# Attention with the fourth step added by a transfer from five probability buffers, and SP's reciprocal work split in two

## The reference

```python
h = _sln(hidden, w, ln_g, ln_b, Wg, bg, Wb, bb)
qkv = (h @ Wqkv.T + bqkv).reshape(B, N, num_heads, hd, 3)      # B 4, N 1024, 16 heads of 32
energy = jnp.einsum('bhqd,bhkd->bhqk', q, k)
att = jax.nn.softmax(energy, axis=-1) / D ** 0.5               # D 512
out = jnp.einsum('bhqk,bhkd->bhqd', att, v)
out = out @ Wp.T + bp
h1 = out + hidden
return _sln(h1, ...) + h1
```

## Time and profile before

| | us |
|---|---|
| median of 3 runs | 1867.25 |
| lowest, highest | 1859.41, 1867.28 |
| profiled execution | 1867.83 |
| its span, first to last instruction | 1865.7 |
| TensorE matmuls busy in the span | 1815.0 |
| VectorE, GpSimd busy | 1252.1, 1217.5 |

### The profile page before, as it was taken

One profiled execution on the slowest core, in us unless ns is written; L12 is line 12 of the kernel. 1 busy time (PEld: TensorE's weight loads), 2 busy tenths in 40 slices (PEclk: granted clock), 3 DMA queues, 4 the chain that ended last, 5 costly groups with the idle time before them and its releaser, 6 DMA issues. The chain is left out here.

```text
span 1865.7 us, 27084 instructions
## 1 busy us (share of the span) xinstructions
PE 1815.0 (97%) x9510; PEld 1214.0 (65%) x9510; DVE 1252.1 (67%) x1986; ACT 836.4 (45%) x1547; POOL 1217.5 (65%) x681
## 2 busy tenths in 40 slices
PE   8999999999999999999999999999999999999897
PEld 4678888888888788888555545554555555454376
DVE  4655655655655565556887777777777777777387
ACT  3223123122223122221476666666666666666465
POOL 2665465465464243332588888888988888898565
PEclk9999999999999999999999999999999999999999
DMA  7410110210103657595877778777878787865796
GB/s 271 118 35 23 57 34 22 56 34 22 56 1 118 209 206 244 180 292 181 199 164 175 184 167 184 175 181 177 182 179 185 172 182 170 185 153 133 232 383 235
DMA packets 135373, 287.10 MB, mean 154 GB/s; under 512 B 23984, under 2 KB 41520, under 8 KB 127200
## 3 DMA queue, kind: packets, MB, share of 16 engines
q1 hardware_dynamic: 102996, 200.10, 35.8%
q0 software_dynamic: 9264, 66.11, 17.4%
q10 hardware_dynamic: 23008, 19.54, 3.3%
HBM read 134.68 MB, written 84.19 MB: 117 GB/s over the span
## 5 line engine op out<-in xcount | busy, mean ns | idle before, releaser
L1619 DVE TENSOR_REDUCE at_mrow<-banks 128x1 f32<-128x512 f32 x976 | 594.1, 681 | 163.7 <-PE banks L1465 163.6
L1715 POOL TENSOR_TENSOR at_sums<-at_probs 128x2048 f32<-128x2048 f32 x127 | 596.6, 4698 | 91.5 <-DMA at_sums<-at_sums 80.2
L1599 ACT ACTIVATE at_probs<-banks 128x512 f32<-128x512 f32 x1024 | 519.7, 621 | 182.7 <-PE banks L1483 177.4
L1465 PE MATMUL banks<-early_ks,early_qs 96*128 96x512 f32 x976 | 407.9, 418 | 11.0 <-DVE at_mrow L1619 7.1
L1483 PE MATMUL banks<-early_qs,early_ks 98*128 98x512 f32 x1024 | 408.0, 417 | 1.8 <-ACT at_probs L1599 1.8
L1465 PEld LDWEIGHTS banks<-early_ks,early_qs 96*128 96x128 f32 x976 | 184.8, 189 | 145.1 <-DVE at_mrow L1619 91.6
L1483 PEld LDWEIGHTS banks<-early_qs,early_ks 98*128 98x128 f32 x1024 | 193.7, 190 | 105.6 <-ACT at_probs L1599 81.5
L1495 PE MATMUL banks<-at_probs,at_v 128*32 128x512 f32 x2048 | 249.1, 603 | 0.7 <-DMA at_v<-v_scratch 0.7
L66 PE MATMUL banks<-l_nt,l_weights 128*128 128x512 f32 x768 | 179.4, 394 | 5.4 <-DVEq L1193 4.3
L66 PE MATMUL banks<-l_ht,l_weights 128*128 128x512 f32 x768 | 178.9, 393 | 1.9 <-issue 1.9
L657 ACT ACTIVATE l_gt<-banks,mod 128x512 f32<-128x512 f32 x60 | 45.1, 778 | 299.3 <-PE banks L526 263.5
(11 more groups left out here) (147 smaller groups left out, 2155.3 us busy)
## 6 DMA issues: line engine op xcount, KB each, us to landing
at_sums<-at_sums POOLq DMA_DIRECT2D x63, 1024.0 KB, 8.3
qk_scratch<-qk_out SPq DMA_DIRECT2D x64, 512.0 KB, 6.1
early_ks<-qk_scratch SPq DMA_DIRECT2D x48, 512.0 KB, 5.2
early_qs<-qk_scratch SPq DMA_DIRECT2D x96, 256.0 KB, 5.7
attn_scratch<-at_out SPq DMA_DIRECT2D x32, 512.0 KB, 7.5
o_a<-attn_scratch SPq DMA_DIRECT2D x32, 512.0 KB, 14.5
chunk_in<-x SPq DMA_DIRECT2D x8, 1024.0 KB, 5.4
v_scratch<-qk_v ACTq DMA_DIRECT2D x32, 256.0 KB, 3.0
```

Of the source, the lines that this page charges most:

```text
L1465: pe.matmul(em[n % 3][:], qs[0:96, slot, half, j, c * P:(c + 1) * P], ks[0:96, slot, j, keys * CH:(keys + 1) * CH], start=True, stop=True) ...
L1599: nc.scalar.activation(probs[:, i % 4, j, :], et[n % 3][:], ACT.Exp).then_inc(exp_done, 1)
L1619: nc.vector.tensor_reduce(mrow[:, half, keys, u:u + 1], em[n % 3][:], AX.X, ALU.max).then_inc(max_done, 1)
L1715: nc.gpsimd.tensor_tensor(into, probs[:, a], probs[:, a + 1], ALU.add).then_inc(pair_ready, 1)
```

## The change

Three things change in attention. (1) Five probability buffers instead of four and two `sums` buffers instead of three. GpSimd's second addition of a quad adds step three to the sum in place, and the transfer adds step four straight from its probability buffer. ScalarE's wait before it fills a buffer again follows: for a buffer that held a fourth step, it waits for that quad's transfer. (2) GpSimd rounds the result right after the product, ahead of the quad's first addition, instead of between the quad's two additions. (3) SP stores the reciprocals (`keep_rden`) ahead of `place_neg`, spreads them (`widen_rden`) behind it, and stores the result behind that.

```diff
@@ -1259,6 +1259,7 @@
         TURN = (SWITCH + PAIRS // 2, SWITCH)
         QUADS = PAIRS // 2
         LAG = 3
+        PROBS_RING = 5
         SPAN = PAIRS // QH
         FRONT = ("M", "E") * 5 + ("E", "M") * 3
         PARTS = 2
@@ -1273,8 +1274,8 @@
         sb("at_stacks_place", [P, 2 * RING * HG * N])
         qs, ks = sh.early_qs, sh.early_ks
         v = sb("at_v", [P, RING, KC, P])
-        probs = sb("at_probs", [P, 4, HG, CH])
-        sums = sb("at_sums", [P, 3, HG, CH])
+        probs = sb("at_probs", [P, PROBS_RING, HG, CH])
+        sums = sb("at_sums", [P, 2, HG, CH])
         av_sb = sb("at_av_sb", [P, QH, CH])
         den_sb = sb("at_den_sb", [P, QH, CH])
         rden = sb("at_rden", [P, QH, CH])
@@ -1333,6 +1334,10 @@
             n = 4 * ((p - SWITCH) % PAIRS)
             return [(whose, at, (n + a) // UNITS, (n + a) % UNITS, keys) for a in range(4) for keys in range(2)]

+        def slot_of(g, i):
+
+            return (STEPS * g + i) % PROBS_RING
+
         def number(g, half, u, keys):

             return 2 * (UNITS * (QH * g + half) + u) + keys
@@ -1398,7 +1403,7 @@
                 sp.dma_start(den_c[:, half],
                              den_sb[0:P:HD, half].rearrange("j (r c) -> j r c", c=DW)).then_inc(den_spread[half], 16)

-            def widen_rden(g, half):
+            def keep_rden(g, half):

                 first = isinstance(g, int) and g == 0
                 sp.wait_ge(rden_ready, halves(g, half))
@@ -1407,6 +1412,10 @@
                     sp.wait_ge(rden_loaded[half], 16 * HG * g)
                 sp.sem_inc(sh.sp_passed, 1)
                 sp.dma_start(sh.rden_d[half].rearrange("j (r c) -> (j r) c", c=DW), rden_c[:, half]).then_inc(rden_stored[half], 16)
+
+            def widen_rden(g, half):
+
+                first = isinstance(g, int) and g == 0
                 sp.wait_ge(rden_stored[half], 16 * (g + 1))
                 if not first:
                     sp.sem_inc(sh.sp_passed, 1)
@@ -1430,18 +1439,20 @@
                 fetch(0)
                 if not first:
                     spread_den(g - 1, 1)
-                    store(g - 1, 0)
+                    keep_rden(g - 1, 1)
                 place_neg(g, slot, 1)
                 if not first:
                     widen_rden(g - 1, 1)
+                    store(g - 1, 0)
                 fetch(1)
                 fetch(2)
                 spread_den(g, 0)
-                if not first:
-                    store(g - 1, 1)
+                keep_rden(g, 0)
                 if with_next:
                     place_neg(g + 1, (slot + 1) % RING, 0)
                 widen_rden(g, 0)
+                if not first:
+                    store(g - 1, 1)
                 fetch(3)

             load_v(0, RING - 1)
@@ -1492,7 +1503,7 @@
                     pe.wait_ge(av_taken, QH * g + i // KC)
                 for j in range(HG):
                     rows = slice(HD * j, HD * (j + 1))
-                    last = pe.matmul(av_ps[rows, :], v[:, slot, kc, rows], probs[:, kc % 4, j, :],
+                    last = pe.matmul(av_ps[rows, :], v[:, slot, kc, rows], probs[:, slot_of(g, i), j, :],
                                      start=kc == 0, stop=kc == KC - 1)
                 last.then_inc(av_done, 1)

@@ -1555,7 +1566,7 @@
             pe.wait_ge(ones_col_ready, 1)
             groups(pe, group)
             pe.wait_ge(pair_ready, PAIRS * G - 1)
-            tiles = [sums[:, (QUADS * G - 1) % 2], probs[:, 2], probs[:, 3]]
+            tiles = [sums[:, (QUADS * G - 1) % 2]] + [probs[:, slot_of(G, i)] for i in (-2, -1)]
             for tile in tiles:
                 for j in range(HG):
                     last = pe.matmul(den_ps[HD * j:HD * (j + 1), :], ones_col[:], tile[:, j, :], start=False, stop=tile is tiles[-1])
@@ -1589,14 +1600,18 @@

             def group(g, slot, nth=None, first=False, load=True, with_next=True):
                 for i in range(STEPS):
-                    if not (first and i < 4):
-
-                        act.wait_ge(av_done, STEPS * g + i - 3)
-                        act.wait_ge(pair_ready, PAIRS * g + (i - 4) // 2 + 1)
+                    if not (first and i < PROBS_RING):
+
+                        old = STEPS * g + i - PROBS_RING
+                        act.wait_ge(av_done, old + 1)
+                        if old % 4 == 3:
+                            act.wait_ge(quad_ready, 16 * (old // 4 + 1))
+                        else:
+                            act.wait_ge(pair_ready, 2 * (old // 4) + (1 if old % 4 < 2 else 2))
                     for j in range(HG):
                         n = HG * (STEPS * g + i) + j
                         act.wait_ge(et_done, n + 1)
-                        nc.scalar.activation(probs[:, i % 4, j, :], et[n % 3][:], ACT.Exp).then_inc(exp_done, 1)
+                        nc.scalar.activation(probs[:, slot_of(g, i), j, :], et[n % 3][:], ACT.Exp).then_inc(exp_done, 1)
                     if g == 1 and i % KC in (3, 5):
                         split_wp(2 * (i // KC) + (i % KC - 3) // 2)
                     if i % KC == KC - 1:
@@ -1698,24 +1713,31 @@
                         for half in range(QH):
                             if pair == SPAN * half:
                                 multiply(g - 1, half)
-                            if pair == SPAN * half + 1:
                                 round_off(g - 1, half)
                             if pair == SPAN * half + 2:
                                 remain(g - 1, half)

                     quad, second = divmod(PAIRS * g + pair, 2)
-                    pool.wait_ge(exp_done, HG * (STEPS * g + 2 * pair + 2))
-                    if second and quad >= 1:
-
-                        pool.wait_ge(quad_ready, 16 * quad)
-                    if not second and quad >= 2:
-
-                        pool.wait_ge(den_done, quad - 1)
-                    into, a = sums[:, 2 if second else quad % 2], 2 * pair % 4
-                    nc.gpsimd.tensor_tensor(into, probs[:, a], probs[:, a + 1], ALU.add).then_inc(pair_ready, 1)
-                    if second:
+                    total = sums[:, quad % 2]
+                    i = 2 * pair
+                    if not second:
+
+                        pool.wait_ge(exp_done, HG * (STEPS * g + i + 2))
+                        if quad >= 2:
+
+                            pool.wait_ge(den_done, quad - 1)
+                        nc.gpsimd.tensor_tensor(total, probs[:, slot_of(g, i)], probs[:, slot_of(g, i + 1)], ALU.add).then_inc(pair_ready, 1)
+                    else:
+
+                        pool.wait_ge(exp_done, HG * (STEPS * g + i + 1))
+                        pool.wait_ge(pair_ready, PAIRS * g + pair)
+                        nc.gpsimd.tensor_tensor(total, total, probs[:, slot_of(g, i)], ALU.add).then_inc(pair_ready, 1)
+                        pool.wait_ge(exp_done, HG * (STEPS * g + i + 2))
                         pool.wait_ge(pair_ready, PAIRS * g + pair + 1)
-                        pool.dma_start(sums[:, quad % 2].rearrange("p j c -> p (j c)"), into.rearrange("p j c -> p (j c)"),
+                        if quad >= 1:
+
+                            pool.wait_ge(quad_ready, 16 * quad)
+                        pool.dma_start(total.rearrange("p j c -> p (j c)"), probs[:, slot_of(g, i + 1)].rearrange("p j c -> p (j c)"),
                                        accum_op=ALU.add).then_inc(quad_ready, 16)


```

## The result

The change made the kernel slower: 1880.14 us (median of 9 executions, 1870.67 to 1886.09) against 1865.16 us before (9 executions), a ratio of 1.0084, 95% interval 1.0071 to 1.0098. The forecast was 1847 us, with a range of 1839 to 1870. The profiled execution of the changed kernel took 1875.40 us, 7.6 us more than that of before, and holds less of the loss than the median does.

A forecast was written before the change was run, and what follows sets the result against it. TensorE's waiting in attention, at most 22.6 us, was taken as what could be won: -13 (reciprocals) -9.6 (denominators and negated maxima) +3 (rows just late) = -20 us, from 1867.25 to 1847 us, range 1839 to 1870.

The forecast's parts named there:

- The floor of 25.86 us a half, 22.6 us to be won: Attention: an unhindered half takes 25.86 us against 26.59 on average, so 22.6 us over 31 halves is waiting.
- The negated rows, the dearest doubt: SP's new order: negated maxima, issued behind the reciprocals' store, land in 3.9 us, costing 3 us in all.
- Rival (a): Negated maxima still land after 6.1 us and become TensorE's bound: +49 us, 1916 us; chance 0.10.
- The five buffers, the wait of ScalarE, the rounding: Transfer lands within ScalarE's 13 us before overwriting, costing nothing; rounding adds 1.1 us to GpSimd, 24.4 of 25.86 us.
- The transfer leaves 1.5 us earlier: GpSimd's second addition no longer waits for the previous transfer, so the accumulating transfer is issued 1.5 us earlier.
- the 13 us of the reciprocals: TensorE's share of VectorE's 20.3 us of reciprocals waiting for spread denominators in attention; 13 us to be won.
- the loads' lead from 7.5 to 8.5 us to 9 to 10 us: SP's loads of the next stack, issued ahead of the negation's end, gain 1.5 us of lead, removing the reciprocals' 13 us.
- Rival (b): Earlier transfer competes with the loads, denominators land as late as now, VectorE stalls: about 1869 us, no change; chance 0.12.
- Rival (c): GpSimd, at 24.4 of 25.86 us, becomes full; late reciprocals delay its additions, half the gain goes: 1857 us; chance 0.08.

The follow-up runs named there:

- forced variant: Changed kernel with the result store moved ahead of the spreading, plus SyncE made to issue the spread denominators about 1 us behind the accumulating transfer: 1963.86 us, ratio 1.0520.
- held-back variant: Changed kernel with GpSimd's accumulating transfer in each half's first quad waiting until SyncE has issued the spread denominators: 1865.66 us, ratio 0.9996.

## Why the prediction was wrong, point by point

- *The floor of 25.86 us a half, 22.6 us to be won*: right. Two variants run at 25.9 us and 1844 to 1846 us.
- *The negated rows, the dearest doubt*: right, and better than taken. They land after 3.5 us (3.9 taken), and no wait of TensorE is for them, although the transfer beside them lands 4.9 us behind the negation on average and not 3. Rival (a) did not come.
- *The five buffers, the wait of ScalarE, the rounding*: right, they cost nothing. No wait of ScalarE is for a transfer, and GpSimd's 80.2 us of waiting for its own are gone. In 44 places its issue waits only for the fourth step's exponentials and comes some 0.5 us behind them, where I had 3.3.
- *The transfer leaves 1.5 us earlier*, worth the 13 us of the reciprocals: right as to the issue, and this is the term that failed. The one near the negation leaves at 4.4 us before it instead of 2.8. It failed twice as a term of the sum. First, "that lifts the loads' lead from 7.5 to 8.5 us to 9 to 10 us": the lead went from 8.0 to 8.3 us only, because the next quad's transfer took 9.3 us to land where I had kept 8.1 (7.7 on average before): the result store, "behind" the negated rows and free there, had come to stand ahead of the next sum's transfer. I had priced what the store leaves and not what it meets. Two kernels bracket this: store out of the way, 1846 us; behind that transfer, 1861 us, one stalled half included.
- Second, the earlier issue was counted as pure gain. The spread denominators are issued 5.5 us before the negation, and the transfer now comes within 1 us of them on average; with a jitter of that size it is sometimes first, and then they lie behind a megabyte (9.6 us to landing, two stalls, 15.5 us in the profile). No rival named it. Held back, 1865.7 us; forced in each half, 1964 us. The trace of before had shown the distance that protected the old order, had I asked what lies behind what. In the half of the earlier trace rows, whose transfer was issued at 1321.69, it is 2.4 us, and in none of the 30 halves is it under 1.1:

```profile
1319.28 0.61 SPq L1398 DMA_DIRECT2D at_den_c<-at_den_sb  x1
```

- *Rival (b), the reciprocals stay late*: its place was right and its reason wrong. I let the transfer compete with the loads; with the store moved and nothing else the reciprocals are on time in 24 of 30 halves, so it was the store that delayed both. Its price, 1869 us, lacked the stalls.
- *Rival (c), GpSimd full*: not in the changed kernel (it waits for ScalarE), but it is what happens under the old order of SyncE, where the product waits 54.8 us.
- The Trainium skill (DMA: Bandwidth & Descriptors, Queues, rings and completion order) has an engine alternate between the queues and drain a whole packet of about 9 to 17 descriptors before it switches. As an estimate from that figure: if a row of 8 KB is one descriptor, the 128 rows of the large transfer are 8 for each of 16 engines, less than one such packet, so whoever comes behind them waits for the whole transfer. The forced variant agrees (none of the small packets in four microseconds of the transfer), the stalled halves of the changed kernel only in part (26 of the 128 in four microseconds in the one, 57 in the other).

What stays open: why some small packets passed in the stalls of the changed kernel and none in the forced variant, why the order of issue still decides where both transfers start only with the end of the loads, and how many halves stall in the executions that have no profile; the held-back variant gives only their sum.

## What to carry to other kernels

Price a moved transfer at both ends: who stood behind it and is free now, and who stands behind it from now on, on the other queues too. An earlier issue is not a gain by itself; write down which small transfer on a critical path is issued around that time, and how many microseconds keep it ahead. If the margin is as small as the jitter, order the two with a semaphore: it cost nothing that could be measured here and took 14.5 us off. And find the pause of the queues (here while the reciprocals landed) before choosing where a large store goes.

## What the runs showed of the hardware that I had not expected

An 8 KB transfer issued 0.2 us behind a 1 MB accumulating one of another queue landed 9.6 us after its issue; in four microseconds of the large one 26 of its 128 packets passed (57 in the other stall, none where it was issued 1.1 us behind). Issued 1.1 us ahead of it, all 128 passed within 0.5 us while the large one was already running. And waits of 2.2 to 3.4 us, repeated each half, already cost clock: at 22 of 29 the granted clock fell (a mean of 0.63 from 1200 to 1204 us), and it was 0.50 after a single wait of 4.35 us. At this kernel a stall cost 1.3 to 1.6 times its length: 4.0 us for 3.1, 6.3 for 5.0 and 9.2 for 5.8.
